# A decoder layer with routed experts on one core: the up layer's bias written into PSUM by VectorE

## What is computed

```
logits = xf @ gate_w.T
scores = jax.nn.softmax(logits, axis=-1)
topk_w, topk_i = jax.lax.top_k(scores, TOP_K)
...
h = jnp.einsum('nd,edh->neh', xf, up_w) + up_b
h = jax.nn.silu(h)
ye = jnp.einsum('neh,ehd->ned', h, down_w) + down_b
y = jnp.einsum('ned,ne->nd', ye, comb).reshape(b, s, d)
```

## Time and profile before

| | |
|---|---|
| median of three runs | 452.72 us (452.65 to 453.34) |
| the profiled execution | 452.99 us, its span 451.2 us |
| PE busy | 437.0 us, 97% of the span |
| VectorE, ScalarE, POOL busy | 304.8, 300.9, 210.9 us |
| mean granted clock of TensorE | 0.993 of full speed |
| tile loop, first up product to last | 340.9 to 425.3 us |

### The profile page before, as it was taken

One profiled execution on the slowest core, in us unless ns is written; L12 is line 12 of the kernel. 1 busy time (PEld: TensorE's weight loads), 2 busy tenths in 40 slices (PEclk: granted clock), 3 DMA queues, 4 the chain that ended last, 5 costly groups with the idle time before them and its releaser, 6 DMA issues.

```text
span 451.2 us, 11055 instructions
## 1 busy us (share of the span) xinstructions
PE 437.0 (97%) x3657; PEld 394.4 (87%) x3657; DVE 304.8 (68%) x1243; ACT 300.9 (67%) x927; POOL 210.9 (47%) x246
## 2 busy tenths in 40 slices
PE   8999999999999999999999999999999999999991
PEld 7888898989989898898988989899889999999970
DVE  3376666787797575868678677969797734333495
ACT  3688666576777668566686665868665686776535
POOL 1899499250103112210237635375733587666521
PEclk9999999999999999999999999999999999999997
DMA  5960121400210001020001214122023654343675
GB/s 147 323 197 3 64 94 46 142 1 1 95 47 1 1 2 36 24 62 23 1 25 59 83 48 118 48 66 76 26 72 96 165 176 141 121 128 118 215 268 196
DMA packets 26543, 40.16 MB, mean 89 GB/s; under 512 B 3199, under 2 KB 17683, under 8 KB 26483
## 3 DMA queue, kind: packets, MB, share of 16 engines
q1 hardware_dynamic: 21532, 27.86, 20.2%
q0 software_dynamic: 3408, 9.33, 5.8%
q10 hardware_dynamic: 1547, 2.27, 1.7%
HBM read 26.83 MB, written 12.61 MB: 87 GB/s over the span
## 4 chain that ended last, share of the span: by engine, by line
PE 86%; DVE 6%; DMA 3%; ACT 1%; issue 1%; POOL 1%; SPq 1%; ACTq 0%; POOLq 0%
PE bank L310 18%; PE bank L311 18%; PE bank L312 18%; PE bank L829 8%; PE bank L879 7%; PE bank L840 7%; DMA ex_raw<-y_dram 2%; PE bank L1033 2%; PE bank L1057 2%; PE bank L780 2%; PE bank L935 1%; PE bank L757 1%; PE bank L1043 1%; PE bank L1065 1%; DVE stats L1581 1%
## 5 line engine op out<-in xcount | busy, mean ns | idle before, releaser
L1219 ACT ACTIVATE probs<-probs,negmax 128x128 f32<-128x128 f32 x256 | 99.7, 393 | 24.6 <-DVE negmax L1493 24.6
L1493 DVE CUSTOM_DVE_ANT_0 probs<-bank,mask 128x128 f32<-128x128 f32 x256 | 62.4, 285 | 45.5 <-PE bank L829 45.5
L310 PE MATMUL bank<-w_hi,ot_hi 128*128 (+1 forms) x284 | 80.6, 284 | 0.1
L311 PE MATMUL bank<-w_lo,ot_hi 128*128 (+1 forms) x284 | 80.3, 283 | 0.0
L312 PE MATMUL bank<-w_hi,ot_lo 128*128 (+1 forms) x284 | 80.1, 282 | 0.0
L1504 DVE TENSOR_TENSOR probs<-probs,rsum 128x512 f32<-128x512 f32 x64 | 58.7, 917 | 2.2
L310 PE MATMUL bank<-xt_hi,w_hi 128*128 128x512 f32 (+1 forms) x148 | 59.7, 403 | 0.0
L611 POOL DMA_INDIRECT xg_dram<-xacc,place x32 | 33.6, 1051 | 54.4 <-PE bank L840 29.6
L311 PE MATMUL bank<-xt_lo,w_hi 128*128 128x512 f32 (+1 forms) x148 | 57.6, 389 | 0.0
L312 PE MATMUL bank<-xt_hi,w_lo 128*128 128x512 f32 (+1 forms) x148 | 57.5, 389 | 0.0
L310 PEld LDWEIGHTS bank<-w_hi,ot_hi 128*128 128x128 f32 x284 | 54.0, 190 | 0.5 <-issue 0.5
(11 more groups left out here) (252 smaller groups left out, 1056.4 us busy)
## 6 DMA issues: line engine op xcount, KB each, us to landing
qkv<-xg_dram SPq DMA_DIRECT2D x39, 128.5 KB, 2.2
ex_raw<-in_w_experts SPq DMA_DIRECT2D x18, 256.0 KB
w_raw<-in_w_quads SPq DMA_DIRECT2D x10, 256.0 KB, 4.7
xacc<-in_x SPq DMA_DIRECT2D x4, 512.0 KB, 4.1
ex_raw<-in_w_cross SPq DMA_DIRECT2D x4, 512.0 KB, 3.9
w_raw<-in_ctx_t_in ACTq DMA_DIRECT2D x4, 512.0 KB, 3.8
w_raw<-in_w_quads SPq DMA_DIRECT2D x3, 512.0 KB, 6.1
xacc<-in_x_t SPq DMA_DIRECT2D x3, 512.0 KB, 6.9
```

Of the source, the lines that this page charges most:

```text
L310: pe.matmul(o, a_hi, b_hi, start=first, stop=False)
L311: pe.matmul(o, a_hi, b_lo, start=False, stop=False)
L1219: nc.scalar.activation(tile, tile, ACT.Exp, scale=-1.0, bias=negmax[:, s.par, h, j:j + 1], accum_out=sums[:, s.par, h, j:j + 1]).then_inc( ...
L1493: nc.vector.tensor_tensor_reduce(probs[:, s.par, h, slices(j, P)], sc_bank[h][:, slices(j, P)], mask[:, :], -SCALE, 3.0e38, ALU.add, ALU.m ...
```

## The change

For tiles 18 to 38 the bias product of the up layer goes. VectorE copies the expert's bias, which lies in every partition, into the tile's PSUM bank (`seed`), and the six products add to what is there (`start=False`). The copy of tile i+1 stands on VectorE in step i behind `tile_h_lo(i - 1)` and the dripped pieces; it waits until Silu of tile i-1 has read the bank (`th_ready`). `tile_up` waits for it (`seeded`). VectorE needs the expert's number in a register, so it loads four at a time from a list of its own, `list_b`, which one more operation makes in `list_later`.

The eight rows of bias are loaded into all partitions, a megabyte in `probs`, by one DMA on ScalarE's queue at the end of slot 32, ahead of `weights_exp` (`load_up_bias`). Since `probs` is taken by it, two buffers of the shared expert's hidden layer (`hid`) go to `qkv`, and one of the landing places of the expert outputs (`yg`) to `xt_hi`. A semaphore that nothing used goes.

```diff
+SEEDED = 18
...
+        list_b = late[:, 3 * D + P + TILES:3 * D + P + 2 * TILES].bitcast(I32)
...
-        hid = [qkv[:, 0:2 * GROUP].rearrange("p (m n) -> p m n", m=2), probs[:, 0, :, :], probs[:, 1, :, :],
-               qkv[:, 0:2 * GROUP].rearrange("p (m n) -> p m n", m=2)]
+        hid = [qkv[:, o:o + 2 * GROUP].rearrange("p (m n) -> p m n", m=2)
+               for o in (0, 5 * GROUP + P, 10 * GROUP, 0)]
+        up_bias = probs[:, :, :, :].rearrange("p a h n -> p (a h n)").rearrange("p (e n) -> p e n", e=NE)
...
                 o = t_up[i % 2][:, 0:D]
+                hi, lo = of_expert(w_hi, e, 0), of_expert(w_lo, e, 0)
+                if i >= SEEDED:
+                    pe.wait_ge(seeded, i - SEEDED + 1)
+                    for k in range(KT):
+                        for a, b in ((xg_hi, hi), (xg_hi, lo), (xg_lo, hi)):
+                            mm = pe.matmul(o, a[:, i % 2, k, :], b[:, slices(k, D)], start=False,
+                                           stop=(k == KT - 1 and a is xg_lo), skip_group_check=True)
+                    mm.then_inc(t_up_done, 1)
+                    return
                 pe.matmul(o, sel[:, 0, :], rows[:, bass.ds(e, 1), :].rearrange("p e n -> p (e n)"),
                           start=True, stop=False)
-                hi, lo = of_expert(w_hi, e, 0), of_expert(w_lo, e, 0)
...
+            def load_up_bias():
+                act.wait_ge(transposed, 2 * SLOTS)
+                act.dma_start(up_bias, up_rows[0:2 * NE, :].rearrange("c p -> (c p)").partition_broadcast(P)
+                              ).then_inc(in_up_bias, 16)
...
-            behind[SLOTS] = [lambda: weights_exp(slice(0, TOK // P - GT)),
+            behind[SLOTS] = [load_up_bias, lambda: weights_exp(slice(0, TOK // P - GT)),
...
+                nc.vector.tensor_scalar(list_b[:, here], tile_e[:, here], float(NE - 1), None, ALU.min)
...
+            def seed(i, e):
+                dve.wait_ge(th_ready, i - 1)
+                if i == SEEDED:
+                    dve.wait_ge(in_up_bias, 16)
+                nc.vector.tensor_copy(t_up[i % 2][:, 0:D], up_bias[:, bass.ds(e, 1), :].rearrange("p e n -> p (e n)")
+                                      ).then_inc(seeded, 1)
...
                     tile_h_lo(i - 1)
                     drip(parts, 2)
+                if SEEDED <= i + 1 < TILES:
+                    seed(i + 1, of_bias.pop(i + 1))
+                if i + 2 >= SEEDED and (i + 2 - SEEDED) % 4 == 0 and i + 2 < TILES:
+                    load_numbers(i + 2)
```

More of the change, by code:

```diff
@@ L184, in decoder_program @@
         scale_last = [[probs_t[:, t, slices(2 * c, P)] for c in range(2)] for t in range(2)]
-        hid = [qkv[:, 0:2 * GROUP].rearrange("p (m n) -> p m n", m=2), probs[:, 0, :, :], probs[:, 1, :, :],
-               qkv[:, 0:2 * GROUP].rearrange("p (m n) -> p m n", m=2)]
+        hid = [qkv[:, o:o + 2 * GROUP].rearrange("p (m n) -> p m n", m=2)
+               for o in (0, 5 * GROUP + P, 10 * GROUP, 0)]
+        up_bias = probs[:, :, :, :].rearrange("p a h n -> p (a h n)").rearrange("p (e n) -> p e n", e=NE)
         crossed = [vv[0][:, slices(half, 2), :] for half in range(2)]
-        held = probs[:, :, :, :].rearrange("p a h n -> p (a h n)")
         marks = staged[:, 2 * GROUP:4 * GROUP]
@@ L198, in decoder_program @@
         yg = [[r.rearrange("p (t n) -> p t n", t=GT) for r in pair] for pair in
-              ((staged[:, 0:2 * GROUP], staged[:, 2 * GROUP:4 * GROUP]), (held[:, 0:2 * GROUP], held[:, 2 * GROUP:4 * GROUP]),
+              ((staged[:, 0:2 * GROUP], staged[:, 2 * GROUP:4 * GROUP]), (xt_hi[:, 0, 0:2 * GROUP].bitcast(F32), xt_hi[:, 1, 0:2 * GROUP].bitcast(F32)),
                (old, ex_raw[:, :, :].rearrange("p a n -> p (a n)")), (qkv[:, 0:2 * GROUP], qkv[:, 2 * GROUP:4 * GROUP]))]
@@ L245, in decoder_program @@
         in_xt0 = [sem(f"in_xt0_k{k}") for k in range(KT)]
-        in_quad = [sem(f"in_quad_{n}") for n in "qkvo"]
+        in_quad = [sem(f"in_quad_{n}") for n in "qkv"]
         q_split, k_split, v_split = sem("q_split"), sem("k_split"), sem("v_split")
@@ L272, in decoder_program @@
         bias_moved = sem("bias_moved")
+        in_up_bias, seeded = sem("in_up_bias"), sem("seeded")
         rows_zeroed, in_up_rows, in_rows, rows_ready = (sem("rows_zeroed"), sem("in_up_rows"), sem("in_rows"),
@@ L1863, in add_shared, with load_numbers @@
                                             ALU.add).then_inc(shared_added, 1)
+            of_bias = {}
+            def load_numbers(i):
+                several = slice(i, min(i + 4, TILES))
+                _, numbers = nc.values_load_multi_w_load_instructions(
+                    list_b[0:1, several], engines=[mybir.EngineType.DVE], min_val=0, max_val=NE - 1,
+                    skip_runtime_bounds_check_because="the list is made of compares that count to at most NE, and a min")
+                of_bias.update(zip(range(several.start, several.stop), numbers))
+            def seed(i, e):
[4 more added lines that the diff above has]
+                                      ).then_inc(seeded, 1)
             def tile_x_lo(i):
```

## The result

The median of the changed kernel is 472.38 us (4 runs, 471.62 to 472.88); the kernel before has 453.03 (4 runs, 452.65 to 454.55). The ratio is 1.0425, 95% interval 1.0405 to 1.0445. The forecast was 470.3 in 463 to 476. The profiled execution of the changed kernel is its fastest, 471.62 with a span of 469.9; that of before is 452.99 with 451.2.

What follows compares the result with a forecast made beforehand. PE bounds the loop before; after the change it waits for VectorE's late copy. 452.99 + 18.05 (tiles 18 to 38) - 0.69 (tail) + 0.2 (bias load) = 470.55, less 0.27 to the median: 470.3 us, range 463 to 476.

Steps and rivals of the forecast that it cites:

- What bounds, and where the copy ends: Tile loop: PE bounds before; the copy behind the low part of h ends at 396.29, PE wants tile 24 at 395.54.
- The next start on VectorE, 0.34: VectorE in the tile loop: its next instruction can start 0.34 us after the low part of h started.
- The register instruction, 0.05: VectorE ahead of each copy: reading the expert number delays the copy by 0.05 us, ends 0 (hidden) and 0.15.
- The copy, 0.41: VectorE's 128x256 fp32 copy of the bias from SBUF into PSUM takes 0.41 us, low end 0.29, high end 0.48.
- PE's restart, 0.21: PE after each copy: wait, slower first product and register instruction cost 0.21 us, low end 0.05, high end 0.31.
- The step, 2.96: Tile loop: each step grows from 2.12 to 2.96 us; over tiles 19 to 37 that adds 15.63 us.
- The tail, -0.69: Behind the tiles: VectorE's 0.69 us wait for a load of expert outputs goes, so -0.69 us (0 at the least).
- The bias load, +0.2: Issue on ScalarE's queue ahead of the last heads' output's high part delays it by 0.2 us (0 to 0.38).
- The saved 21 products: PE, tiles 18 to 38: 0.12 us each, 2.5 us if PE stayed the bound, lie in its stall and bring nothing.
- The clock rival: PE's idle time in each step lowers TensorE's clock to 1.2 GHz: 16 us more, 486 us; chance 0.06.
- Free bias: Rival: VectorE's copy ends ahead of PE in each step, so 2.5 us less, 450.4 us; chance 0.04.
- paid once: Rival: only the first seed is late, later tiles keep the old step less the bias product: 451.2 us; chance 0.02.

Runs made afterwards that it cites:

- kernel 1: The changed kernel with VectorE's copy for tile i+1 and the load of its numbers first in step i, ahead of the low part of x: 452.72 us.
- kernel 2: The changed kernel with the copy and the load of numbers between the low part of x and the low part of h: 464.19 us.
- kernel 4: The changed kernel with a copy of 32 columns in place of 256, at the same place: 467.77 us.
- kernel 7: The changed kernel plus a small product at fixed addresses, its result unused, that carries PE's wait for the copy: 472.92 us.
- kernel 5: Kernel 1 with PE reading its expert numbers one tile earlier, behind the up products of the tile before: 451.70 us.

## Why the prediction was right

- **What bounds, and where the copy ends** (right). The forecast rested on VectorE's program order: the copy behind the low part of h cannot end before PE wants tile i+1. The trace shows that order, and kernels 1 and 2 show that the place alone makes the loss: 452.7, 464.2 and 472.4 us for first, second and last in the step.
- **The next start on VectorE, 0.34** (right): 0.33 to 0.34 between the three instructions.
- **The register instruction, 0.05** (too much): it takes 57 ns, but the copy starts 0.33 after the low part of h. It is hidden, the low end that was named.
- **The copy, 0.41** (right): 417 ns. The Trainium skill (VectorE: DVE Perf Modes, section "Why PSUM operands drop a tier") has one element per cycle for fp32 with an operand in PSUM. The 224 columns that kernel 4 takes off are worth 233 ns, 1.04 ns per column, and the 417 ns for 256 columns lie 268 ns, 1.05 per column, under the copy of 512 columns out of PSUM. So the two copies that touch PSUM share one rate, which agrees; the double rate that VectorE's cast between SBUF tiles suggested does not hold here.
- **PE's restart, 0.21** (the term that was mis-sized): the first product starts 0.24 after the copy's end and the second 0.22 after that, so 0.24 + 0.10 = 0.34, just past the high end of 0.31. The row it was taken from the earlier trace rows has a wait at fixed addresses. In kernel 7, with the wait at fixed addresses too, 0.10 of the 0.24 goes; that leaves 0.14 against 0.05 in that row, where VectorE wrote to SBUF and not to PSUM, and no run settles this last 0.09.
- **The step, 2.96**: 3.04. Register -0.06, copy +0.01, restart +0.13 make +0.08, which over 19 steps is the 1.5 us by which the loop ran over (+17.17 against +15.63). **Tile 18** +0.93 against +0.84 and **tile 38** +1.61 against +1.58 carry the same. In the profiled executions the time is 1.1 us over the forecast, less than the 1.7 of all steps: the -0.37 ahead of tile 18, which no term foresaw, and the 0.2 of the bias load that did not come make up for part of it, which is luck.
- **The tail, -0.69** (right): -0.75, of which 0.60 is the gap that closes ahead of the row below. The expert additions of the tail no longer wait for a transfer; the row that answers to the last of the earlier trace rows is

```profile
453.63 1.67 DVE L1956 SCALAR_TENSOR_TENSOR xacc<-ex_raw,w_raw,xacc 128x256 f32<-128x256 f32 x4
```

- **The bias load, +0.2** (wrong, the low end of 0 held): the last heads' high part starts 0.19 later than in the earlier trace rows, at 317.61, but the same 0.18 already stands between the two executions at 312.5, ahead of the load's issue at 315.17, and a like 0.18 at 161 us. So the issue of 0.35 us is hidden under ScalarE's running instruction.

```profile
315.17 0.35 ACTq L1274 DMA_DIRECT2D probs<-up_rows  x1
315.22 0.59 ACT L1235 ACTIVATE probs_t<-bank 128x512 f32<-128x512 f32 x1
```

- **The saved 21 products** (right): they lay in PE's stall and brought nothing. Where the stall is taken away and the reads are moved (kernel 5) the loop gains 2.57 us, 2.4 of it from 20 of them, and the time 1.2.
- **The clock rival** (refuted): PE worked 74% of each step for 56 us and the granted clock stayed at 1.00, the 2.4 GHz level. Window, PE busy, the other engines, clock, DMA:

```profile
384.00:440.00 56.00, 41.66 (x319) 38.06 (x319) 19.80 (x55) 27.82 (x86) 24.23 (x36) 1.00 0.33 104
```

The rule of the Trainium skill on frequent short idles, which the prediction weighed (TensorE: Matmul & The Clock Gate, section "A second HAM failure mode: psum-queue depth-cycling"), does not show here: some 18 idles of 0.8 us, bank after bank, left the granted clock at 1.00. **Free bias** and **paid once** fell with the step; kernel 1 shows that the first of them was a matter of order alone. It also shows that its price was wrong: 450.4 leaves out what PE's reads and the tail take back.

## What to carry to other kernels

Work that goes from a full engine to an idle one is free only if its place in the idle engine's order lies ahead of the wait where that engine idles; a total of idle time (1.35 us a step here) doesn't tell where it lies. Draw the chain from the freed buffer to the next product, and put the moved write at the first point at which its buffer is free. And when a product goes from the row of the bounding engine, look at what it was covering: here register reads took back 1.7 of the 2.5 us in kernel 1, and with these moved a tail that waits for transfers still took back half in kernel 5 (1.38 of 2.57 in its profiled execution).

## What the runs showed of the hardware beside that

- One small VectorE operation is long at one place of the program. The 128x4 operation, whose median is 0.165 us, takes 1.00 to 1.03 us there in eight of the ten kernels' executions, that of before among them, and 0.50 and 0.48 in those of the changed kernel and kernel 1; no run explains it. With the 0.18 of the last point (-0.50 and +0.18) it makes up most of the -0.37 ahead of tile 18.

```profile
324.76 1.00 DVE L1593 TENSOR_SCALAR var_eps<-mv 128x4 f32<-128x4 f32 x1
```

```profile
324.95 0.50 DVE L1609 TENSOR_SCALAR var_eps<-mv 128x4 f32<-128x4 f32 x1
```

- PE's read of four numbers into registers takes 0.3 to 1.2 us of its sequencer. Of that, some 0.1 us reached the products with the bias products in place, some 0.4 without them, and nothing at most places when the read stood one tile earlier; what decides it was not shown.
- The same instruction before the tile loop starts up to 1.7 us apart between executions of kernels that are alike up to there (312.2 to 313.9 for one of VectorE's), so differences of a microsecond in single executions were read from within the loop, not from the span. Before and changed kernel were 0.18 apart there.
